# Four subtractions of the last attention moved from VectorE (DVE) to GpSimd (POOL)

## What is computed

```python
def step(carry, jkv):
    m, l, o = carry
    s = jnp.einsum('bqd,bkd->bqk', q_i, k_j) * SCALE
    s = jnp.where(kpos > qpos, -jnp.inf, s)
    m_new = jnp.maximum(m, s.max(-1))
    p = jnp.exp(s - m_new[..., None])
    l_new = l * jnp.exp(m - m_new) + p.sum(-1)
    ob = jnp.einsum('bqk,bkd->bqd', p, v_j)
    o = o + (ob - o) * (l / l_new)[..., None]
    return ((m_new, l_new, o), None)
```

## Time and profile before

| | |
|---|---|
| median of 3 runs | 3992.66 us |
| lowest and highest | 3991.66 and 3997.45 us |
| the profiled execution's own time | 3994.44 us |
| its span, first to last instruction | 3992.6 us |
| PE, DVE, ACT, POOL busy | 90%, 65%, 45%, 15% |
| mean granted TensorE clock | 0.936 of full speed |

### The profile page before, as it was taken

How to read it: one execution, slowest core, us unless ns; L and a number is a source line. 1 busy time by engine, 2 the same in 40 slices (tenths; PEclk the granted TensorE clock), 3 DMA queues, 4 the chain that set the end, 5 groups by cost and what they waited for, 6 DMA issues and landing times.

```text
span 3992.6 us, 66986 instructions
## 1 busy us (share of the span) xinstructions
PE 3586.5 (90%) x20335; PEld 2096.9 (53%) x20335; DVE 2576.8 (65%) x6166; ACT 1802.0 (45%) x4300; POOL 608.3 (15%) x1188
## 2 busy tenths in 40 slices
PE   3799998999999899999989999998999999899974
PEld 2355554555555455555555555555555555555542
DVE  5464766667676766767676676767666666765553
ACT  0354544445454444545544454554445455444521
POOL 1020302102030210303021030302103030110201
PEclk7799998989999898999999899999999999999975
DMA  5020202002020200202020020202002020200000
GB/s 98 4 25 4 25 2 31 2 13 19 6 27 2 31 2 7 25 5 27 2 31 2 7 25 5 27 2 31 2 12 20 5 28 2 31 2 4 1 3 3
DMA packets 51980, 59.15 MB, mean 15 GB/s; under 512 B 19634, under 2 KB 41076, under 8 KB 51572
## 3 DMA queue, kind: packets, MB, share of 16 engines
q0 software_dynamic: 23040, 37.91, 9.8%
q1 hardware_dynamic: 11636, 7.87, 0.8%
q10 hardware_dynamic: 16896, 8.39, 0.7%
HBM read 11.27 MB, written 4.19 MB: 4 GB/s over the span
## 4 chain that ended last, share of the span: by engine, by line
PE 79%; DVE 9%; issue 6%; ACT 3%; POOL 2%; DMA 1%; SPq 1%; ACTq 0%; DVEq 0%; POOLq 0%
PE ps L1325 13%; PE ps L1282 6%; PE ps L1339 6%; PE ps L1293 6%; PE ps L1346 5%; PE ps L1305 5%; PE ps L1433 4%; PE ps L1418 4%; PE ps L1399 4%; PE ps L1273 3%; PE ps L1519 3%; PE ps L1497 3%; PE ps L1354 3%; PE ps L1513 1%; PE ps L1420 1%
## 5 line engine op out<-in xcount | busy, mean ns | idle before, releaser
L681 ACT ACTIVATE share_a<-ps,nma 128x128 f32<-128x128 f32 (+3 forms) x1024 | 539.1, 528 | 547.2 <-DVE nma L976 536.3
L1325 PE MATMUL ps<-share_g,xnTd 128*128 128x128 f32 (+3 forms) x2048 | 757.7, 467 | 30.6 <-ACT share_a L681 16.7
L976 DVE TENSOR_REDUCE nma<-ps 128x1 f32<-128x128 f32 (+3 forms) x1024 | 490.7, 488 | 397.9 <-PE ps L1327 382.5
L727 ACT ACTIVATE share_z<-ps 128x512 f32<-128x512 f32 (+1 forms) x704 | 369.3, 558 | 497.4 <-PE ps L1420 494.2
L1041 DVE TENSOR_REDUCE nmx<-ps 128x1 f32<-128x384 f32 (+3 forms) x704 | 427.0, 635 | 122.7 <-PE ps L1401 117.9
L1325 PEld LDWEIGHTS ps<-share_g,xnTd 128*128 128x128 f32 x2048 | 343.0, 198 | 267.7 <-issue 138.7
L947 DVE SCALAR_TENSOR_TENSOR share_g<-share_g,ps 128x512 f32<-128x512 f32 x256 | 175.3, 685 | 405.3 <-ACT share_g L694 403.4
L550 POOL TENSOR_TENSOR vn<-va,rla 128x256 f32<-128x256 f32 x256 | 160.3, 627 | 1277.7 <-DVE rla L937 1277.5
L1282 PE MATMUL ps<-xnTd,mg 128*128 128x512 f32 x512 | 307.4, 685 | 23.1 <-ACT va L655 23.1
L1293 PE MATMUL ps<-share_a,vn 128*64 128x512 f32 (+3 forms) x2048 | 309.8, 445 | 18.3 <-POOL vn L550 18.3
L577 POOL TENSOR_TENSOR share_s<-q1T,tab 128x1024 f32<-128x1024 f32 x16 | 30.4, 1899 | 1768.7 <-ACT q1T L755 1768.7
(11 more groups left out here) (220 smaller groups left out, 6002.9 us busy)
## 6 DMA issues: line engine op xcount, KB each, us to landing
qst<-share_r POOLq DMA_DIRECT2D x144, 128.0 KB, 7.3
kst<-share_r POOLq DMA_DIRECT2D x144, 128.0 KB, 12.7
xin<-in_L_attn_x ACTq DMA_DIRECT2D x16, 256.0 KB, 2.7
out<-xn ACTq DMA_DIRECT2D x16, 256.0 KB, 2.3
wgv<-in_L_ffn_expert_wv SPq DMA_DIRECT2D x1, 2048.0 KB
qst<-share_h SPq DMA_DIRECT2D x48, 16.0 KB, 2.4
tab<-in_constants SPq DMA_DIRECT2D x1, 520.0 KB
share_a<-in_L_attn_W_K SPq DMA_DIRECT2D x1, 512.0 KB
```

Of the source, the lines that this page charges most:

```text
L681: activation(pa[:, h % 4, OFF[t]:OFF[t] + P * (t + 1)], ps[:, pos % 3, 0:P * (t + 1)], ACT.Exp, bias=nma[:, h, t:t + 1], accum_out=la[:, h ...
L727: activation(pt[:, n % 2, h % 4:h % 4 + k, 0:wd], src, ACT.Exp, scale=SCALE_B)\
L976: v.tensor_reduce(nma[:, h, t:t + 1], ps[:, pos % 3, 0:P * (t + 1)], AX.X, ALU.max, negate=True).then_inc(amax, 1)
L1325: mm(ps[:, b, 0:P * (t + 1)], xnTd[:, tile(t)], gs[:, h % 2, 0:P * (t + 1)], start=True, stop=False)
```

## The change

The four subtractions go from DVE's `shift1` to a new `shift1` on POOL, at the same places of the table. A new semaphore, `rm_ready`, is raised by the last instruction of the running maximum, and POOL waits for it before each subtraction. DVE's `shift1` keeps the decay difference, at k = 3, and now waits for `rm_ready` itself; the step count of DVE's own chain falls from 81 to 80.

```diff
-BEHIND_STEPS = 81
+BEHIND_STEPS = 80
...
+                def shift1(k):
+
+                    pool.wait_ge(rm_ready, count(prv, BEHIND["rm_ready"], 1))
+                    two = ss[:, 2 * k:2 * k + 2, :, :].rearrange("p a b k -> p (a b) k")
+                    peak = rm[:, 2 * k:2 * k + 2, :].rearrange("p a b -> p (a b)")
+                    nc.gpsimd.tensor_tensor(two, two, peak.unsqueeze(2).to_broadcast(
+                        [P, 2 * NFB, FLASH]), ALU.subtract).then_inc(sub1_ready, 1)
...
-                        link_b(v.tensor_tensor(dst[:, :, near:NFB], src[:, :, near:NFB], src[:, :, 0:NFB - near],
-                                               ALU.max))
+                        ins = v.tensor_tensor(dst[:, :, near:NFB], src[:, :, near:NFB], src[:, :, 0:NFB - near],
+                                              ALU.max)
+                        if near < 4:
+                            link_b(ins)
+                        else:
+                            ins.then_inc(rm_ready, 1)
 
                 def shift1(k):
-                    two = ss[:, 2 * k:2 * k + 2, :, :].rearrange("p a b k -> p (a b) k")
-                    v.tensor_tensor(two, two, wide(rm[:, 2 * k:2 * k + 2, :]).unsqueeze(2).to_broadcast(
-                        [P, 2 * NFB, FLASH]), ALU.subtract).then_inc(sub1_ready, 1)
                     if k == 3:
+                        dve.wait_ge(behind_step, count(prv, BEHIND_STEPS, b_steps[0]))
+                        dve.wait_ge(rm_ready, count(prv, BEHIND["rm_ready"], 1))
                         v.tensor_tensor(dm[:, :, 1:NFB], rm[:, :, 0:NFB - 1], rm[:, :, 1:NFB], ALU.subtract)\
                            .then_inc(dm1_ready, 1)
```

More of the change, by code:

```diff
@@ L90 @@
     xn2_ready=4, xn2T_psum=1, xn2T_ready=1, kqv1_psum=3, kq1_ready=2, v1_ready=1, qbd_ready=1, s1_psum=8,
-    s1_ready=8, sub1_ready=4, dm1_ready=1, fac1_ready=1, p1_ready=4, co_ready=1, pw1_ready=4, sum1_ready=4, totals_ready=1, ratios_ready=1, pT1_psum=8,
+    s1_ready=8, rm_ready=1, sub1_ready=4, dm1_ready=1, fac1_ready=1, p1_ready=4, co_ready=1, pw1_ready=4, sum1_ready=4, totals_ready=1, ratios_ready=1, pT1_psum=8,
     pT1_ready=8, o1_psum=2, om_ready=2, oT1_ready=1, pr1_psum=1, pr1_added=1, xq_ready=1, xqT_psum=1, xqT_ready=1,
@@ L421, in build_layers @@
         s1_ready = sem("s1_ready")
+        rm_ready = sem("rm_ready")
         sub1_ready = sem("sub1_ready")
@@ L611, in run @@
                 walk(dict(split_q=lambda: send_stack(0), split_k=lambda: send_stack(1),
-                          spread_queries1=spread_queries1, totals1=totals1,
+                          spread_queries1=spread_queries1, shift1=shift1, totals1=totals1,
                           blend1=blend1, weigh1=weigh1), dense, i, nxt, prv)
```

## The result

The changed kernel takes 4002.74 us (median of 12 runs, 3997.99 to 4008.55); beside it the kernel before took 3992.64 us (12 runs, 3989.71 to 3997.45). The ratio is **1.0026, 95% interval 1.0017 to 1.0035**: the change costs 10 us, a quarter of a per cent. The forecast was 4000.5. The profiled execution of the changed kernel took 4006.05 us, with a span of 4004.2 us and a mean granted clock of 0.935. Ratios and verdicts leave three slow executions out: 5342.76 and 6817.38 us of the kernel before (in the session of the idle ACT copy, the unused POOL work and the first subtraction earlier) and 9498.77 us of the last of these; the median of 3994.55 us given beside these three would be 3994.16 without them.

What follows compares the result with a forecast made beforehand. PE bounds the kernel (3586.5 of 3992.6 us busy), waiting for ACT at the place, with DVE's subtractions on the path. 10.2 - 3.0 + 0 + 0.6 = +7.8 us gave 4000.5 us; range 3992 to 4008.

Steps and rivals of the forecast that it cites:

- sign of being wrong: Prediction is wrong if pass length moves otherwise than PE's step behind the va copy, or a POOL DMA stand changes.
- Subtraction on POOL: Each of the four subtractions takes POOL 1.90 us, 1.86 from the second on, 7.47 for four in a row.
- rival 4: POOL's subtraction is longer than its multiplication, 2.1 us each, 0.7 to 0.9 more per pass; 4011 us; chance 0.05.
- One ordinary pass, +0.85: ACT waits for POOL's subtractions; the va copy comes 0.80 us later, PE ends 0.85 late; bounds 0.4 to 1.3.
- The decay difference gets in between: DVE's decay difference, issued during POOL's third subtraction, runs before the fourth, which may cost exponential 4 0.2 us more.
- rival 1: Decay difference stands until POOL's last subtraction ends, 0.45 us more in each of 12 passes; 4006 us; chance 0.20.
- Twelve such passes: Eleven loop passes and the one after the loop share the ordinary pattern: 12 x 0.85 = +10.2 us.
- Rival 2: No slower: ACT's waits overlap small idle spots, an ordinary pass loses 0.3 us or less; 3992.7 us; chance 0.20.
- rival 3: Faster: emptier DVE queues let dense maxima through earlier, needing 1 us a pass; 3982 us; chance 0.05.
- Collisions, -3.0: Two passes where POOL and DVE collide get between 1.0 and 1.9 us shorter: 2 x 1.5 = -3.0 us.
- The pass with POOL's stand, 0: Pass at 1337.36, POOL's queue standing among its DMA issues: both ends within half a microsecond, taken as 0.
- The drain, +0.6: Last attention with nothing beside it: POOL's four subtractions take 7.47 us, making exponential 4's sum +0.6 us later.

Runs made afterwards that it cites:

- idle ACT copy: Kernel before plus an ACT copy of 512 elements, used by nothing, between exponential 3 and the copy of va; 4003.55 against 3994.55 us, ratio 1.0026.
- unused POOL work: Changed kernel plus an unused POOL multiplication of 512 elements ahead of the four subtractions; 4026.51 against 3994.55 us, ratio 1.0077.
- first subtraction earlier: Changed kernel with POOL's first subtraction put ahead of the normalisation of head 3; 3998.91 against 3994.55 us, ratio 1.0004.
- new wait alone: Kernel before with all subtractions still on DVE, only its wait for the running maximum changed to `rm_ready`; 3996.71 against 3993.97 us, ratio 1.0008.

## Why the prediction was right or wrong

The forecast of 4000.5 us lies 2.2 below the median, the median lies inside the range, and the sign was right. That its sum, +7.8, is so near to +10 is partly luck. Two errors cancelled: the terms at the place were too large (+7.8 against 4.6), and about 5 us elsewhere were left out. Its own sign of being wrong, that the pass length moves otherwise than PE's step, did come.

- **Subtraction on POOL.** 1.90 us once and 1.86 in a row, from the same engine's multiplication: measured 7.48 us for four. Right; rival 4 falls. The Trainium skill, GPSIMD Engine Reference, section 3.1, with its ratio of 1.96, would have made it an estimated 2.4 us. The rows of after decide against that here: 1.90 against 1.24 is 1.53.
- **One ordinary pass, +0.85.** The mechanism is right: ACT waits for POOL's subtractions by name, the copy of va goes back and PE's wait grows. The size was not: +0.60. The step that failed is the start of the chain, "Exponential 1 starts at 2778.15 as before". The change also takes away DVE's stand behind the last running-maximum step, which I had not counted as a part of it. POOL's normalisation, and with it all four subtractions, start 0.17 us earlier, exponential 3 comes at +0.60 and not +0.80, and exponential 4 at +0.7 and not +1.05. The run with the new wait alone shows the missing part by itself.
- **The decay difference gets in between.** Right as to DVE: 0.39 us in the ordinary pass, where rival 1 had 2 us; rival 1 falls. The 0.2 us that this was to cost the fourth subtraction did not appear: POOL needs 7.48 us with it, and 7.47 for its four multiplications without. In the kernel with the first subtraction earlier the difference does stand, for 1.53 us, and costs 0.21: the rival's mechanism exists and depends on when DVE comes to it.
- **Twelve such passes.** All twelve have the step: 12 x 0.60 = 7.2 us (7.3 as measured) instead of 10.2. Rival 2 wanted 0.2 or less a pass and falls; rival 3 wanted a gain and falls.
- **Collisions, -3.0.** Measured -3.2, -2.1 and -1.8 in the three traces. The place and the cause are right. Of six passes three lie within the bounds of 1.0 to 1.9, one just above, and two below (0.88 and 0.68); in these two the clock fell behind a wait of 2.77 us for the copy of va, a wait that the prediction did not count in a colliding pass. Both passes also scatter by 0.6 us between traces of the unchanged kernel.
- **The pass with POOL's stand, 0.** Measured -0.42 in all three. The kernel before scatters there from 0 to -0.94, so its sign isn't certain. The stands themselves stayed in the same passes with the same lengths.
- **The drain, +0.6.** Right to the hundredth: the totals begin 37.99 us after the marker before and 38.59 after. It does not reach the end as such: what follows the last marker is 0.1, 2.6 and 2.6 us shorter than before in the three traces, with the low clock in other places of it. Timeline of POOL and DVE there, beside the earlier trace rows:

```profile
3893.69 7.48 POOL L587 TENSOR_TENSOR share_s<-share_s,rm 128x1024 f32<-128x1024 f32 x4 [26.73 <-DVE rm L1124]
3903.65 0.21 POOL L595 TENSOR_TENSOR cc<-ll,dm 128x8 f32<-128x8 f32 x1 [2.49 <-DVE ll L1140]
...
3893.72 1.95 DVE L1135 TENSOR_TENSOR dm<-rm 128x56 f32<-128x56 f32 x1
```

- **Not in the sum at all: the clock at the ends of the passes, about +5 us.** Why it comes with the change stays open. The prediction took it for granted that "ordinary passes" would be 231.8 instead of 231.0 us. There is no such one length: in the kernel before, three markers follow each other at 1578.85, 1812.48 and 2043.86, two ordinary passes of 233.6 and 231.4 us, by what the clock does. By the sum of the places alone the kernel would be 4.6 slower, at about 3997 and below my forecast; with the low clock's share it is at 4003, above it.

## What to carry to other kernels

Before moving an instruction to a slower engine, look at who waits for its first two results, not at how busy the engines are: here the first subtraction could be moved for nothing, and the second made the path longer. Count a wait that the move makes unnecessary as a part of the change, even when it is only 0.2 us of an engine's own chain. And where the granted clock moves between its levels within a pass, price a delay in PE's path with a margin: its length is the lower end, and where the clock fell behind the wait here it was two to three times that.

## What the chip did that I had not expected

- **A jump in the price of a wait.** In one and the same place PE waited 1.03, 1.54 and 1.63 us with the clock staying full behind it in every ordinary pass; at 1.87 us it fell in four of twelve, and at 2.63 us in eleven. With 2.63 us the step was 3.3 us in most of them, for a wait 1.6 longer than before.
- **The same end of a pass, with more or less of it at half clock.** 10.2 or 23.9 us, with PE's waits the same to 0.2 us in the two passes shown, make a difference of 4.4 us in a pass of 231.
- **The shared access lets a waiting instruction in between two of the other engine.** The decay difference took 0.39 us when it was issued at the end of a subtraction, and 1.95 us in the drain, where it came 0.03 us after the start of one; POOL's four lost nothing to it. In the colliding pass and in the kernel with the first subtraction earlier it was issued 0.20 and 0.44 us into POOL's last one and took 1.76 and 1.53 us. The Trainium skill, SBUF — State Buffer, section "Who interferes with whom", calls the shared access an exclusive lock and has a DVE instruction with two SBUF inputs contend with a GpSimd one that reads SBUF. The trace agrees: 1.95 us for an instruction that takes 0.21 alone, beside a subtraction of 1.90.
